# Two batches in one PSUM bank, twice: bank sharing in the spectra and the gate stage of a four-stage kernel, with a new order of work

## What is computed

```python
q, kv = (x @ W_q.T), (x @ W_kv.T)            # 16 heads of 16; FFT along the head
qf, kvf = l2_normalize(fft(q)), l2_normalize(fft(kv))
values = ifft(qf * cumsum(kvf, axis=tokens)).real @ W_o.T          # block 1
gate = sigmoid(slope * (score(x) - center))  # 8 experts, best one per token
block2 = (1 - g) * x + g * (bias[e] + dgn[e] @ (upd[e] @ (x - debias[e])))
attn = softmax(Q K^T / 4) V @ W_o.T          # block 3, 16 heads of 16, 256 tokens
h = relu(x @ w1.T) ** 2                      # block 4, w1 and w2 made ternary
y = rms_norm(h) @ w2.T
```

## Time and profile before

| | before |
|---|---|
| median of 3 runs | 843.16 us (842.44 to 843.82) |
| profiled execution: its own time | 849.45 us |
| profiled execution: span | 847.4 us |
| busy: TensorE, VectorE, ScalarE, GpSimd | 689.9, 603.5, 442.9, 410.6 us |
| mean granted TensorE clock | 0.917 |
| DMA: share of 16 engines, moved | 34.4%, 59.63 MB |

### The profile page before, as it was taken

How to read it: one execution, slowest core, us unless ns; L and a number is a source line. 1 busy time by engine, 2 the same in 40 slices (tenths; PEclk the granted TensorE clock), 3 DMA queues, 4 the chain that set the end, 5 groups by cost and what they waited for, 6 DMA issues and landing times.

```text
span 847.4 us, 14775 instructions
## 1 busy us (share of the span) xinstructions
PE 689.9 (81%) x5100; PEld 530.8 (63%) x5100; DVE 603.5 (71%) x1429; ACT 442.9 (52%) x897; POOL 410.6 (48%) x601
## 2 busy tenths in 40 slices
PE   4326657798999999999999999999999998878663
PEld 3214535565767676767686868686868685746452
DVE  2974449496979797979797979797979796734020
ACT  0113122448575757575757575757575746572530
POOL 3121111115464646464646464646464645364564
PEclk9557677799999999999999999999999999999866
DMA  6100080616171617161616161616161616250000
GB/s 191 62 0 14 0 149 11 140 14 137 15 150 20 144 15 149 20 144 15 149 22 142 16 150 22 143 22 143 22 142 16 135 23 129 38 115 14 1 13 12
DMA packets 298170, 60.57 MB, mean 71 GB/s; under 512 B 237352, under 2 KB 293616, under 8 KB 298096
## 3 DMA queue, kind: packets, MB, share of 16 engines
q1 hardware_dynamic: 298096, 59.63, 34.4%
HBM read 38.38 MB, written 20.97 MB: 70 GB/s over the span
## 4 chain that ended last, share of the span: by engine, by line
PE 45%; DVE 36%; issue 6%; POOL 4%; ACT 4%; SPq 3%; DMA 3%; POOLq 0%; DVEq 0%; ACTq 0%
DVE nmax L1235 10%; PE pC L728 7%; PE pA L512 5%; PE pC L706 5%; DVE x L1040 4%; PE pS L681 3%; PE pA L539 3%; DVE spec L1079 3%; PE pA L498 3%; DVE ss L1069 2%; PE pS L631 2%; PE pB L605 2%; PE pA L555 2%; PE pA L589 2%; PE pA L570 2%
## 5 line engine op out<-in xcount | busy, mean ns | idle before, releaser
L1235 DVE TENSOR_REDUCE nmax<-pB 128x2 f32<-128x512 f32 x256 | 165.5, 675 | 21.8 <-PE pB L605 20.3
L861 ACT ACTIVATE pt<-pS 128x512 f32<-128x512 f32 x256 | 149.1, 608 | 12.4 <-PE pS L631 12.4
L631 PE MATMUL pS<-qT,kT 98*128 98x256 bf16 x512 | 92.6, 277 | 12.8 <-ACT pt L861 10.9
L605 PE MATMUL pB<-kT,qT 96*128 96x256 bf16 x512 | 96.6, 282 | 7.4 <-DVE nmax L1235 4.3
L1444 POOL TENSOR_TENSOR hid_lo<-hh,hid 128x512 fp32r<-128x512 f32 x64 | 81.8, 1279 | 6.1 <-POOL hh L1416 5.3
L1416 POOL TENSOR_TENSOR hh<-hr 128x512 f32<-128x512 f32 x64 | 72.4, 1132 | 20.2 <-ACT hr L889 20.1
L824 ACT COPY qkv<-pA 128x512 f32<-128x512 f32 x48 | 30.2, 630 | 93.6 <-PE pA L589 93.6
L706 PE MATMUL pC<-x3T,w1T 128*128 128x256 f32 x256 | 71.2, 309 | 6.5 <-DVE x3T_lo L1291 4.2
L1421 POOL TENSOR_TENSOR hsum<-hsum,hsq 128x512 f32<-128x512 f32 x48 | 60.9, 1270 | 30.1 <-ACT hsq L901 30.1
L657 PE MATMUL pO<-pt,v_ext 128*32 128x256 f32 x1024 | 70.3, 393 | 2.8 <-ACT pt L861 2.8
L1355 POOL TENSOR_SCALAR vea<-mva 128x2 f32<-128x2 f32 x16 | 3.6, 223 | 131.6 <-DVE mva L1036 131.6
(11 more groups left out here) (175 smaller groups left out, 1765.9 us busy)
## 6 DMA issues: line engine op xcount, KB each, us to landing
qk_scratch<-qk_part SPq DMA_DIRECT2D x48, 256.0 KB, 5.1
qT<-qk_scratch SPq DMA_DIRECT2D x96, 128.0 KB, 3.0
kT<-qk_scratch SPq DMA_DIRECT2D x96, 128.0 KB, 2.8
xa<-in_x SPq DMA_DIRECT2D x16, 256.0 KB, 3.1
v_scratch<-qkv SPq DMA_DIRECT2D x16, 256.0 KB, 3.7
v_heads<-v_scratch SPq DMA_DIRECT2D x16, 256.0 KB, 3.5
out_y<-y SPq DMA_DIRECT2D x16, 256.0 KB, 3.6
pt<-in_wfc SPq DMA_DIRECT2D x1, 1024.0 KB, 7.6
```

The source lines that it names most:

```text
L605: ins = pe.matmul(pB[h % 2][:, s * T:(s + 1) * T], qT[k][0:STACK, u * P:(u + 1) * P], kT[k][0:STACK, h * T:(h + 1) * T], start=True, stop= ...
L631: ins = pe.matmul(pS[h % 2][:, s * T:(s + 1) * T], kT[k][:, u * P:(u + 1) * P], qT[k][:, h * T:(h + 1) * T], start=True, stop=True)
L861: act.activation(pt[:, (h // 4) % 2, h % 4].rearrange("p s n -> p (s n)"), pS[h % 2][:], ACT.Exp, scale=HD ** -0.5).then_inc(S["probs"], 1)
L1235: dve.tensor_reduce(nmax[:, h * SIDES:(h + 1) * SIDES], pB[h % 2][:].rearrange("p (s k) -> p s k", s=SIDES), AX.X, ALU.max, negate=True).t ...
```

## The change

1. **Bank pA0 (spectra).** a_xt of a batch no longer waits for a_res1 of the batch before, only for that of two before (attn_read, back=2), and in the second batch for the first one's proj_sb; a_cum waits for both proj_sb of the next batch (for the last batch, for attn_read of the batch before). So the next batch's turning and projection use the bank before the running sum of this one.
2. **raw_spec is double**, one for even and one for odd batches; a_proj_sb waits for products of two batches before, in place of attn_ready of the one before; a_squares waits for crossed in place of prt_ready. The transposed products no longer go to the second half of raw_spec: prodT is now prod itself.
3. **Bank pA1 (gate and projection).** g_x1t waits for ffn_read (g_res2) of the batch before in place of its last qkv_sb; g_mixt waits for that qkv_sb; g_x2t waits for gate_read of the next batch. So gate of one batch, x2 and projection of the batch before, and mix of the first take turns in the bank.
4. The squares of x1 that feed s2 are written to mix in place of x2, so two waits (xb_copied, x2t_ready) go. minus_half shrinks to SIDES columns.
5. **The order table** is new on all engines.

```diff
@@ -97,36 +97,41 @@
-    "c_hid_1 e_score_5 e_score_6 g_mixt c_hid_2 e_score_7 g_mix e_score_8 e_out_1 e_score_9 e_score_10 "
...
+    "e_score_8:+1 g_x1t e_out_1:+1 e_score_9:+1 e_score_10:+1 g_gate b_max_0:+1 b_max_1:+1 e_score_11:+1 "
...
@@ -184,13 +189,13 @@
...
         ones = sb("ones", [P, P])
-        minus_half = sb("minus_half", [P, 2 * UNITS])
+        minus_half = sb("minus_half", [P, SIDES])
 
...
         xT_lo = sb("xT_lo", [P, SIDES, CH, P], F32R)
-        raw_spec = sb("raw_spec", [P, SIDES, 512])
+        raw_spec = [sb(f"raw_spec{k}", [P, SIDES, 512]) for k in range(2)]
         ss = sb("ss", [P, SIDES, 32])
@@ -270,7 +275,7 @@
...
 
-        prodT = raw_spec[:, 1, :]
+        prodT = prod[:].rearrange("p s c n -> p (s c n)")
         onT = oS[:, 0:2, :].rearrange("p g n -> p (g n)")
@@ -501,8 +506,10 @@
...
                 pe.wait_ge(S["x_in"], nth(i, PER["x_in"], 16))
-                if has(i):
-                    pe.wait_ge(S["attn_read"], before(i, PER["attn_read"]))
+                if has(i, 2):
+                    pe.wait_ge(S["attn_read"], before(i, PER["attn_read"], back=2))
+                elif has(i):
+                    pe.wait_ge(S["proj_sb"], before(i, PER["proj_sb"]))
                 four_transposes(pA[0], xa[k]).then_inc(S["xt_ready"], 1)
@@ -524,6 +531,10 @@
...
                 pe.wait_ge(S["spectra"], nth(i, PER["spectra"], 2))
+                if i + 1 < BATCHES:
+                    pe.wait_ge(S["proj_sb"], nth(i + 1, PER["proj_sb"], 2))
+                else:
+                    pe.wait_ge(S["attn_read"], before(i, PER["attn_read"]))
                 for r in range(SIDES):
@@ -543,7 +554,7 @@
...
                 if has(i):
-                    pe.wait_ge(S["qkv_sb"], before(i, PER["qkv_sb"]))
+                    pe.wait_ge(S["ffn_read"], before(i, PER["ffn_read"]))
                 four_transposes(pA[1], x1[k]).then_inc(S["x1t_ready"], 1)
@@ -558,6 +569,8 @@
...
                 pe.wait_ge(S["mix_done"], nth(i, PER["mix_done"], 1))
+                if has(i):
+                    pe.wait_ge(S["qkv_sb"], before(i, PER["qkv_sb"]))
                 for s in range(SIDES):
@@ -572,6 +585,8 @@
...
                 pe.wait_ge(S["x2_done"], nth(i, PER["x2_done"], 2))
+                if i + 1 < BATCHES:
+                    pe.wait_ge(S["gate_read"], nth(i + 1, PER["gate_read"], 1))
                 four_transposes(pA[1], x2).then_inc(S["x2t_ready"], 1)
@@ -769,18 +784,18 @@
...
 
-            def a_proj_sb(i, s):
+            def a_proj_sb(i, k, s):
                 act.wait_ge(S["proj_ready"], nth(i, PER["proj_ready"], s + 1))
                 if s == 0:
-                    if has(i):
-                        act.wait_ge(S["attn_ready"], before(i, PER["attn_ready"]))
-                act.copy(raw_spec[:, s, :], pA[0][:]).then_inc(S["proj_sb"], 1)
+                    if has(i, 2):
+                        act.wait_ge(S["products"], before(i, PER["products"], back=2))
+                act.copy(raw_spec[k][:, s, :], pA[0][:]).then_inc(S["proj_sb"], 1)
 
...
                 if has(i):
-                    act.wait_ge(S["prt_ready"], before(i, PER["prt_ready"]))
-                act.activation(spec[:].rearrange("p s a b n -> p (s a b n)"), raw_spec[:].rearrange("p s n -> p (s n)"),
+                    act.wait_ge(S["crossed"], before(i, PER["crossed"]))
+                act.activation(spec[:].rearrange("p s a b n -> p (s a b n)"), raw_spec[k][:].rearrange("p s n -> p (s n)"),
                                ACT.Square).then_inc(S["squares"], 1)
@@ -790,14 +805,10 @@
...
                 act.copy(flat(x1T[:]), pA[1][:]).then_inc(S["x1t_sb"], 1)
-                if has(i):
-                    act.wait_ge(S["xb_copied"], before(i, PER["xb_copied"]))
-                if has(i):
-                    act.wait_ge(S["x2t_ready"], before(i, PER["x2t_ready"]))
                 for s in range(SIDES):
...
                         act.wait_ge(S["x1_sq"], nth(i, PER["x1_sq"], s))
-                    act.activation(x2[:, s, :], x1[k][:, s, :], ACT.Square,
+                    act.activation(mix[:].rearrange("p s n -> p (s n)"), x1[k][:, s, :], ACT.Square,
                                    accum_out=s2[:, s:s + 1]).then_inc(S["x1_sq"], 1)
@@ -914,7 +925,7 @@
...
             for n in range(SIDES):
-                steps[f"a_proj_sb_{n}"] = lambda i, k, n=n: a_proj_sb(i, n)
+                steps[f"a_proj_sb_{n}"] = lambda i, k, n=n: a_proj_sb(i, k, n)
             for n in range(2):
@@ -1074,15 +1085,15 @@
...
 
-            def a_spectra(i, s):
+            def a_spectra(i, k, s):
                 dve.wait_ge(S["norm_rs"], nth(i, PER["norm_rs"], 1))
...
                     spec[:, s].rearrange("p c q (h k) -> p c (q h) k", k=BINS),
-                    raw_spec[:, s, :].rearrange("p (c m k) -> p c m k", c=2, k=BINS),
+                    raw_spec[k][:, s, :].rearrange("p (c m k) -> p c m k", c=2, k=BINS),
                     rn[:, s, :].rearrange("p (a m b) -> p a m b", a=1, b=1).broadcast_to([P, 2, 32, BINS]),
...
 
-            cross = raw_spec[:, 0, :].rearrange("p (s c n) -> p s c n", s=SIDES, c=2)
+            cross = [v[:, 0, :].rearrange("p (s c n) -> p s c n", s=SIDES, c=2) for v in raw_spec]
 
@@ -1095,19 +1106,19 @@
...
                 dve.tensor_tensor(prod[:], spec[:, :, :, 0, :], cum, ALU.mult).then_inc(S["crossed"], 1)
-                dve.tensor_tensor(cross[:, :, 0], spec[:, :, 0, 0, :], cum[:, :, 1, :], ALU.mult
+                dve.tensor_tensor(cross[k][:, :, 0], spec[:, :, 0, 0, :], cum[:, :, 1, :], ALU.mult
                                   ).then_inc(S["crossed"], 1)
-                dve.tensor_tensor(cross[:, :, 1], spec[:, :, 1, 0, :], cum[:, :, 0, :], ALU.mult
+                dve.tensor_tensor(cross[k][:, :, 1], spec[:, :, 1, 0, :], cum[:, :, 0, :], ALU.mult
                                   ).then_inc(S["crossed"], 1)
 
-            def a_products(i, n):
+            def a_products(i, k, n):
                 if n == 0:
...
                     dve.wait_ge(S["products"], nth(i, PER["products"], 1))
-                    dve.tensor_tensor(tail(prod[:, :, 1]), tail(cross[:, :, 0]), tail(cross[:, :, 1]),
+                    dve.tensor_tensor(tail(prod[:, :, 1]), tail(cross[k][:, :, 0]), tail(cross[k][:, :, 1]),
                                       ALU.add).then_inc(S["products"], 1)
@@ -1320,8 +1331,8 @@
...
             for n in range(2):
-                steps[f"a_spectra_{n}"] = lambda i, k, n=n: a_spectra(i, n)
-                steps[f"a_products_{n}"] = lambda i, k, n=n: a_products(i, n)
+                steps[f"a_spectra_{n}"] = lambda i, k, n=n: a_spectra(i, k, n)
+                steps[f"a_products_{n}"] = lambda i, k, n=n: a_products(i, k, n)
                 steps[f"b_maxt_{n}"] = lambda i, k, n=n: b_maxt(i, n)
```

8 lines of the change are left out of this document (6 added, 2 removed), and 47 rows, old and new, of the table ORDER.

## The result

The changed kernel takes 855.63 us (median of 4 runs, 855.21 to 856.61), the one before 843.45 beside it: a ratio of 1.0143, 95% interval 1.0118 to 1.0168. It is slower, where 836.2 was forecast. The profiled execution took 855.21 us, its span is 853.1.

The account below looks back on a forecast made before the run. It took a serial ring of waits between VectorE and TensorE, not one engine, as the bound. Fill 251, ten turns 414, drain 167 and tail 8.4 gave span 840.4, 7.0 less; 843.2 - 7.0 = 836.2 us, range 812 to 858.

Parts of the forecast that it names:

- Fill: Start to c_res of batch 0: shorter turns but more depth, 251 us, 16 us later than before.
- rival 1: The fill's turns stay as long as before: batch 5 at 275 us, 855 us in all; chance 0.15.
- Full turn: One pass through the order table with every stage at work: 41.4 us against 42.33, ten of them 414.
- the holds: VectorE instructions made to wait beside POOL's hidden layer work: seven meetings, 3.4 us a turn.
- the ring: Chain from c_y through VectorE and TensorE to the next c_y: closes at 41.4 us, 38.0 without meetings.
- Late loads: SP's q and k loads delay b_max_0 by at most 2.4 us a turn; 1.5 gives 851 us; chance 0.10.
- Rival 2: VectorE beside POOL becomes the bound, deciding from 4.3 us of meetings; at 5.0 a 43.0 us turn, 852; chance 0.17.
- Rival 3: TensorE alone decides the full turn, meetings being short: turn 39.35 us, 816 us in all; chance 0.18.
- Drain: The last five turns, without a stage: 37, 36, 35, 30, 29 us, 167 against 180.4, 13 saved.
- the depth: From a_xt of a batch to its c_y, 6.3 turns instead of 5.0; costs time only in fill and drain.
- Base: Starting time 843.2 us, the median of runs before, less 7.0 us of span saved (847.4 to 840.4).
- Sign: Chances for the whole kernel: faster 0.58, same 0.08, slower 0.34.

Follow-up runs that it names:

- b16: The kernel before, unchanged with 16 batches, run and profiled a second time: span 841.4 us, ratio 1.0008.
- a_keep: Changed kernel with 12 unused matmuls on constants in each turn without an a stage: 849.79 us, ratio 1.0049 to the kernel before.
- a_gs: Changed kernel with two gate steps earlier on VectorE and the store of y behind the q and k loads: 843.50 us, ratio 0.9969 to before.
- a_gate: Changed kernel with g_gate1_4 and g_gate1_5 right behind g_gate1_3 on VectorE: 845.15 us, ratio 1.0001 to the kernel before.
- d_act: a_gs with hidden layer work ahead of some scores in the turns to batches 11 to 15: ratio 0.9963 to the kernel before.
- a_late: Changed kernel with d_act's order only in the turns to batches 13 to 15: 851.15 us, ratio 1.0082 to the kernel before.
- e_fill: a_gs with 12 filler matmuls on constants in each of the turns to batches 10 and 11: ratio 0.9934 to the kernel before.
- b_keep: The kernel before with the same filler matmuls as a_keep in its drain: ratio 1.0017 to the kernel before unchanged.
- e_best: a_gs with d_act's order in the turns to batches 13 to 15 and e_fill's filler: median 833.95 us, ratio 0.9834 to before.

## Why the prediction was wrong

Its span was 840.4 us and is 853.1, 12.7 more. By its own terms:

- **Fill, right in size.** a_res1 of batch 0 at 74.0 (76), turns of 30.6, 35.1, 36.8, 37.9, 40.3 (30, 32, 38, 39, 41), batch 5 at 254.8 (256), c_res of batch 0 at 250.4 (251). The fill's turns did get shorter, so rival 1 falls; the fill still cost 17.5 us against b16, by depth and by the later first a_res1, which no run sets apart. The parts that the prediction names for the first turn add up to 27.7 and not to its 30; the turn took 30.6, so 3 us of it are unnamed.
- **Full turn, right.** 41.1 against 41.4. Inside, the holds were right (3.0 for 3.4 us), but the plain turn is 40.4, so the ring was priced 1.0 us too long. Late loads, which I had counted as just in time, gave back some 0.5 a turn, and the low clock in the turn to 10 (43.1 us, 40.9 in a_keep at full clock) 0.2 more: that the sum came within 0.3 is in part luck. Rival 2 was there in kind and below the point from which it decides. Rival 3 was nearly reached only with the gate steps moved: turns of 39.7 in a_gs and in three of a_gate's.
- **Drain, wrong: the step that failed.** "I take 37, 36, 35, 30, 29": measured 40.4, 39.6, 37.4, 35.1, 30.7, 16.2 us more. I priced a turn by the stages that are absent from it, and credited the depth ("e is half done a turn earlier"). But the turns to 13, 14 and 15 are a chain: c_res, the hidden layer's first parts behind the scores, 13 us of GpSimd, c_ms, e_wo, c_y. None of it is in the absent stages, and no part of it is shorter for depth. In after the turn to 14 has 13.6 us ahead of GpSimd's part, 13.4 of it and 8.1 behind; 30 was forecast, and 30.9 in d_act is the least seen. Before's own drain, 177 in b16, already shows that chain (8.7, 14.8 and 10.6 us). The second part of the step is the clock: the turns to 10, 11 and 12 I took at full clock, and they ran at 0.92, 0.92 and 0.87. That is 2.2 us in each of the turns to 10 and 11 by a_keep, and 2.6 in that to 12 by the runs in which it had 0.95; in the turns to 13 and 14 it has a share too, by d_act and a_late. How much of the 16.2 us is chain and how much clock, no run separates in full.
- **Base, wrong.** 6.7 of the 19.4 us of the miss are no part of the kernel. I took off what the profiled execution of before stood above its median, and set the forecast at its span less 4.2 us. After's median is 2.5 above its span. b16 shows that the first profile of before was long in fill and drain by 6 us; a fresh forecast doesn't inherit that. From 840.4 and the 2 to 2.5 us that an execution has around its span, 842.4 to 842.9 would have come out, or no change.
- **Sign.** Measured against b16, the balance is +17.5 in the fill, -12.0 in the full turns, +6.2 in the drain. The gain a turn, 1.2 us, was forecast at 0.9; a loss of 16 us in the fill had been seen. The forecast of faster hung on 13 us saved in the drain alone, and for its turns no row had been read but their sum.

## What to carry to other kernels

Depth in a software pipeline is paid once in fill and drain and earned back once a turn: multiply the gain of a turn by the full turns before anything else, and run the kernel at two batch counts to see both numbers apart. Price the turns of a drain along their own chain, read from the drain of the kernel before, and at the clock that its rows show, never by taking absent work off a full turn. An order that is tuned for the full turn can have its own variant for the last turns, and tiny VectorE steps should stand where GpSimd's instructions are short.

## What the hardware showed

- A VectorE instruction of 16 columns took 1.16 us beside GpSimd's hsum and 0.25 where GpSimd stood in root steps, and it ended with GpSimd's instruction (391.04 and 391.00). Setting two such steps elsewhere took 0.7 us off most full turns, though two later ones and spec were then held longer.
- 12 more matmuls in each of two turns (e_fill) raised the granted clock there from 0.92 to 1.00 and made them 5.3 us shorter. They were of use only where TensorE was still busy most of the turn; in the thinner turns of a_keep and b_keep they gained nothing.
- The same instructions in the same turn took some 37.0 or 39.6 us (to batch 12, five kernels at 0.95 and three at 0.87) and 34.3 or 37.2 us (to batch 13, at 0.95 and 0.86). Executions of e_best reach from 827.6 to 843.1 us, those of before beside it from 842.1 to 849.4. Three of e_best's take 827.6 to 828.8 us at a mean granted clock of 0.919 to 0.924, the other three 839.1 to 843.1 at 0.899 to 0.905; how much of that is such turns was not traced.
- One store of 0.5 us of SP's time, ahead of the q and k traffic, showed as up to 1.6 us of TensorE waiting for kT.
